# Spreading the side work of a merged four-layer kernel over the attention steps, and group norm two steps earlier

## The reference

```
x = x + L0(gn(x))   # an mLSTM block plus a linear branch, a 3x3 convolution, batch norm, leaky relu
x = x + L1(gn(x))   # attention with 6 heads
x = x + L2(gn(x))   # deformable depthwise 3x3
x = x + L3(gn(x))   # 1x1 to 510, patch transform 2x2, depthwise 3x3, gelu gate, 1x1 back

L1: xq = tokens @ preproj.T + b;  theta = pi * tanh((xq - mean) / std)     # 6 angles for a token
    zq, zk = expectation values of two 6-qubit circuits on theta
    q, k = layernorm(zq @ Wq.T), layernorm(zk @ Wk.T)                        # 4 values each
    attn = softmax(-(|q|^2 + |k|^2 - 2 q.k) / tau)                           # 1024 x 1024 for a head
    out = gate * attn @ v
L2: offsets = conv3x3(x);  out = sum over 9 taps of w[c, tap] * bilinear(x, position + offset[tap])
```

## Time and profile before

| | us |
|---|---|
| median of 3 runs | 8774.78 (8744.1 to 8776.88) |
| profiled execution | 8783.56 |
| its span, first to last instruction | 8781.7 |
| mean granted TensorE clock | 0.922 |
| TensorE busy (matmul) | 7681.9 |
| VectorE busy | 5722.6 |
| ScalarE busy | 3843.6 |
| GpSimd busy | 2158.7 |

### The profile page before, as it was taken

One profiled execution on the slowest core, in us unless ns is written; L12 is line 12 of the kernel. 1 busy time (PEld: TensorE's weight loads), 2 busy tenths in 40 slices (PEclk: granted clock), 3 DMA queues, 4 the chain that ended last, 5 costly groups with the idle time before them and its releaser, 6 DMA issues.

```text
span 8781.7 us, 99875 instructions
## 1 busy us (share of the span) xinstructions
PE 7681.9 (87%) x37116; PEld 3793.0 (43%) x37116; DVE 5722.6 (65%) x9725; ACT 3843.6 (44%) x7430; POOL 2158.7 (25%) x1798
## 2 busy tenths in 40 slices
PE   7999999999999957798988888888888988888877
PEld 4555555555555522344344344343343343343343
DVE  4676666676676734676676676675676676676664
ACT  4555555555555525434435425434334434344320
POOL 1122222222222200214213224123124123133152
PEclk9999999999999978798898999998998999999989
DMA  1111111111111120344434444444444444444365
GB/s 64 37 37 42 46 49 43 40 37 42 43 53 43 37 72 4 103 114 149 130 104 156 125 116 153 130 117 153 116 132 153 115 133 153 110 133 150 110 189 140
DMA packets 244228, 850.01 MB, mean 97 GB/s; under 512 B 46412, under 2 KB 49176, under 8 KB 243360
## 3 DMA queue, kind: packets, MB, share of 16 engines
q1 hardware_dynamic: 150272, 388.71, 16.4%
q0 software_dynamic: 92160, 453.06, 16.3%
q10 hardware_dynamic: 1312, 1.87, 0.1%
HBM read 602.10 MB, written 89.68 MB: 79 GB/s over the span
## 4 chain that ended last, share of the span: by engine, by line
PE 43%; DVE 12%; issue 4%; ACT 4%; DMA 3%; SPq 1%; POOL 0%; another core or an unknown queue 0%; ACTq 0%; DVEq 0%; POOLq 0%
PE ps L2246 9%; PE ps L2481 5%; PE ps L2698 5%; DVE arena L1931 4%; PE ps L2235 4%; PE ps L389 3%; PE ps L2677 3%; PE ps L2168 2%; PE ps L2709 2%; PE ps L2152 2%; PE ps L2365 2%; DMA arena<-img,arena 1%; PE ps L2211 1%; SPq L2732 1%; PE ps L2463 1%
## 5 line engine op out<-in xcount | busy, mean ns | idle before, releaser
L2514 POOL DMA_INDIRECT arena<-img,arena x1152 | 1361.1, 1181 | 2889.2 <-DMA img<-arena 1744.6
L2409 DVE SCALAR_TENSOR_TENSOR arena<-arena 128x384 f32<-128x384 f32 x1152 | 750.0, 651 | 571.6 <-DMA arena<-img,arena 524.8
L1931 DVE TENSOR_REDUCE arena<-ps 128x2 f32<-128x1024 f32 x768 | 894.7, 1217 | 329.6 <-PE ps L2211 326.7
L2090 ACT ACTIVATE arena<-ps 128x512 f32<-128x512 f32 x1536 | 827.3, 600 | 507.5 <-PE ps L2235 341.0
L2246 PE MATMUL ps<-arena 128*64 128x512 f32 x3072 | 904.1, 671 | 0.0
L998 POOL TENSOR_TENSOR arena<-arena 128x512 f32<-128x512 f32 x384 | 443.8, 1162 | 1761.1 <-DMA arena<-decay 1760.8
L2698 PE MATMUL ps<-arena 128*64 128x512 f32 x3072 | 793.3, 639 | 72.2 <-ACT arena L2658 38.2
L2481 PE MATMUL ps<-arena 128*96 128x128 f32 x4608 | 608.9, 289 | 139.3 <-DVE arena L2398 139.3
L2481 PEld LDWEIGHTS ps<-arena 128*96 128x96 f32 x4608 | 557.6, 173 | 321.7 <-issue 319.9
L2235 PE MATMUL ps<-arena 32*128 32x512 bf16 x1536 | 409.5, 409 | 188.1 <-issue 121.9
L964 PE MATMUL ps<-arena 128*128 128x512 f32 x1152 | 507.2, 596 | 0.0
(11 more groups left out here) (349 smaller groups left out, 12720.7 us busy)
## 6 DMA issues: line engine op xcount, KB each, us to landing
arena<-arena SPq DMA_DIRECT2D x1024, 144.5 KB
arena<-decay SPq DMA_DIRECT2D x384, 256.0 KB, 3.2
img<-arena SPq DMA_DIRECT2D x162, 384.0 KB, 2.6
arena<-img,arena POOLq DMA_INDIRECT x1152
arena<-y SPq DMA_DIRECT2D x16, 768.0 KB, 6.4
arena<-x SPq DMA_DIRECT2D x16, 768.0 KB
out<-arena SPq DMA_DIRECT2D x16, 768.0 KB
arena<-x SPq DMA_DIRECT2D x16, 512.0 KB, 5.1
```

Source lines behind the costliest of these rows:

```text
L1931: dve.tensor_reduce(out, self.wides[B.at("max", b, g, n, h) // 2].rearrange("p (a b) -> p a b", a=2), AX.X, AL.max).then_inc(*S.mark("max_ ...
L2090: act.activation(self.p[n % 6], B("score", b, n)[:, :], ACT.Exp).then_inc(*S.mark("p_act", b, n))
L2409: dve.scalar_tensor_tensor(gb[:, 0:384], gb[:, 384:768], pp[:, 1, n:n + 1], gb[:, 0:384], AL.mult, AL.add).then_inc(*S.mark("corner_x", b, n))
L2514: pool.indirect_dma_start(self.g[n % 6], None, img, bass.IndirectOffsetOnAxis(ap=ii[:, n:n + 1], axis=0)).then_inc(*S.landed(f"{self.tag}g ...
```

## The change

Five numbers move, and the digits of PACE. The group norm of the next image is stepped from t = 44 on, no longer from t = 46, on all three engines. `dve_add` goes from t = 44 to t = 42, `act_affine` from t = 40 to t = 38, where it comes behind `finish(0)`. In PACE the sums over all 128 steps stay as they were (185, 155, 172), and in the string of images 2 to 14 also those up to steps 8 and 88; the digits of steps 1 to 7 (in the strings of images 2 to 14 and of the last), of steps 78 to 85 and of steps 88 to 127 are new. From t = 14 on there is one side step for each step (in the last image two from t = 37 on). No instruction is added or removed.

```diff
@@ Layer1.dve
             if t == 39:
                 finish(0)
-            if t == 44:
+            if t == 42:
                 self.dve_add(dve, b + 1)
-            if t > 45:
+            if t > 43:
                 next(gn, None)
@@ Layer1.act
             if t == 38:
                 finish(0)
-            if t == 40:
+            if t == 38:
                 self.act_affine(act, b + 1)
-            if t > 45:
+            if t > 43:
                 next(gn, None)
@@ PACE
 PACE = ("0304040433303700013600007001109209996000400000000007020621002011"
-        "2053100202000000033643000000000000002411100100901000000412000010",
-        "0202020222201010201423061000504220400010401121212314223330012011"
-        "1331111003000000033300000000082000200411100101710100000403000002",
-        "0202020222200020101234070200043200320123000222112134223321012011"
-        "1502111021000000034270000010000000241330013320500100300501100074")
+        "2053100202000012230000001111111111111111111111111111111111111110",
+        "0112111122201010201423061000504220400010401121212314223330012011"
+        "1331111003000022230000001111111111111111111111111111111111111110",
+        "0112111122200020101234070200043200320123000222112134223321012011"
+        "1502111021000022230000001111111111111111111111122222222222222222")
```

## The result

The changed kernel took 8823.62 us (median, 8790.02 to 8853.5), the kernel before beside it 8785.15 (8744.1 to 8803.38): ratio 1.0047, interval 1.0033 to 1.0062. So the change costs about half a per cent, 38 and 47 us by the medians. The forecast was 8775 us, no change; the range up to 8850 holds the time.

The account below looks back on a forecast made before the run. TensorE, busy 87% of the span, was taken as the bound, with ScalarE and VectorE interlocked in the merged stage. Terms of +0.1 us per image x14 and -4 for image 0 gave -3 in total; forecast 8775 us, range 8715 to 8850.

Parts of the forecast that it names:

- Row blocks earlier: Blocks from t = 4: TensorE waits 1.6 us for the slopes, less regained ring waits; +0.4 us per image, ends -0.9 and +1.9.
- score 31 to next L2115: Attention step 31 to the next image's first transposes: 44.8 us after, 41.4 before, +3.4 per image.
- L2115 to the variance matmul: Next image's start: first transposes find the full clock, so 13.9 us becomes 11.5.
- The first twelve steps: Image's head: a gather issued before L1867 and one corner less bring weigh 4 1.3 us earlier, ends -0.3 and -2.
- image 0: No side work, no weigh to wait for: idle 3.16 us becomes some 1.3, the clock stays up, -4 us once.
- regained ring waits: Row blocks: pairs avoid the waits of threes for their ring of buffers, 0.81 us, with ScalarE's share about 1.2.
- Steps 31 to 44, the new wait: At t = 44 TensorE waits about 5.2 us for weigh 2, bounded by 2 and 8.7.
- The clock: Behind the wait at t = 44 the granted clock falls, costing 3 us more per image, ends 0 and 3.9.
- The image's end: Group norm output comes about 1 us after TensorE's work, before 3.16 us idle; bank wait +0.8; L434's total below 20 us.
- A: Rival, gain without its price: the clock stays up at t = 44; 8722 us; with its kin 0.28.
- B: Rival: the wait at t = 44 grows to 8.7 us and the clock costs 3.9; 8834 us; with its kin 0.30.
- C: Rival: the effect is swallowed by remote waits during the run of gathers and measures as nothing; chance 0.15.

Follow-up runs that it names:

- e11: Changed kernel plus unused matmuls in both new TensorE waits, three at t = 4 and ten at t = 44: 8720.87 us, ratio 0.9963 to the kernel before.
- e1: Changed kernel with the row blocks put back to three each at t = 7, 8, 9: 8756.29 us, ratio 0.9999 to the kernel before.
- e6: Changed kernel plus ten unused matmuls in the wait for weigh 2 at t = 44, on another chip: 8539.58 us, ratio 1.0033 to the kernel before.
- e3: Kernel before with only the change's new step numbers (42, 38, 43), PACE digits as before: 8752.17 us, ratio 0.9998 to the kernel before.
- e8: Changed kernel with blocks and weigh 2 moved back, plus four unused matmuls in two layer 3 places, other chip: 8469.14 us, ratio 0.9955 to the kernel before.
- e12: Changed kernel with row blocks back at t = 7 to 9 and weigh 2 ahead of finish(0): 8686.36 us, ratio 0.9924 to the kernel before.
- e5: Changed kernel with row blocks back at t = 7 to 9 and weigh 2 ahead of finish(0), other chip: 8457.7 us, ratio 0.9933 to the kernel before.
- e7: Changed kernel plus three unused matmuls in the wait for the slopes at t = 4, on another chip: 8575.52 us, ratio 1.008 to the kernel before.

## Why the prediction came out as it did

The time is inside the range, 0.5 to 0.6% above the kernel before where the forecast said none. Most of the sum's terms hold; one fails. With a loss of 0.5 to 0.6% the time lies at the border between "no change" (0.42) and "slower by over 0.5%" (0.30). Measured values are the table's, changed against before in its two pairs of columns:

```
us per image                 forecast   measured      ends given
Row blocks earlier             +0.4    +3.7, +3.6    -0.9 to +1.9
score 31 to next L2115         +3.4    +2.3, +2.4
L2115 to the variance matmul   -2.4    -2.8, -2.8
  the last two together        +1.0    -0.6, -0.4    -2 to +5.4
The first twelve steps         -1.3    -1.7, -1.6    -2 to -0.3
sum of the parts touched       +0.1    +1.4, +1.6
image 0, once                  -4      -2.3, -2.6
```

**Row blocks earlier** is the step that failed. The idle time was as forecast, 1.58 us for 1.6, in all 16 places where L2463 waits. Two things were priced wrong. First, the regained ring waits, 1.2 us: they were read from image 6, and most images have less of them. In the kernel before, 7 of the 13 images have no idle time over 0.3 us at their blocks (image 7 is one, first row below; the earlier trace rows has image 6 with 0.81), and where the clock stays up the stretch has a mean of 17.2 us, only 0.6 above those without a wait (16.6). Of the 26 images in both profiles of the changed kernel the clock stayed up in five, and there it takes 18.3 to 19.6 us, mean 19.0; e11, whose clock always stays up here, has 18.64. So without the clock the term is +1.4 to +1.8: as good as nothing was regained, which by the prediction's own terms makes +1.6 (the end of +1.9 that it gives doesn't follow from them).

Second, the clock: in the other 21 images the stretch takes 19.7 to 23.6 us, most often 22.7, which adds some 2 us to the mean. The prediction looked for a fall of the clock only behind idle stretches of over 3 us, the ones its rows showed, and gave the 1.58 us none. The trace of the kernel before had the sign at the blocks themselves: in image 8 it fell behind 1.83 us (the timeline row and the window of 2 us below; busy, clock, DMA share, GB/s), in image 10 behind 1.29 us. e1 shows the whole term: back at 17.56, and 0.5% of the kernel with it.

```profile
5623.99 2.51 PE L2463 MATMUL ps<-arena 96*128 96x96 f32 x24
...
5959.20 0.55 PE L2463 MATMUL ps<-arena 96*128 96x96 f32 x4 [1.83 <-ACT arena L2443]
```

```profile
5960.00:5962.00 2.00, 2.00 (x9) 0.60 0.82 326
```

The Trainium skill (TensorE: Matmul & The Clock Gate, section A second HAM failure mode: psum-queue depth-cycling) tells of a kernel in which TensorE's micro-idles between groups of matmuls came often enough to make the clock swing. That short idle times can bring the clock down is borne out at t = 4; here a single one of 1.58 us in an otherwise busy stretch was enough, in 21 of 26 images. The prediction had used another section of that page (HAM oscillation), and only for what a fall costs, not for what brings one.

**Steps 31 to 44, the new wait** held: 5.08 us for 5.2, at t = 44, with VectorE behind `finish(0)` and `dve_add`. The total for L2398 is 199.3 us (forecast some 190). **The clock** behind it was put at 3 us; e6 and e11, which hold it up, get 2.0 to 2.3 from t = 31 to L2115; in the next stretch e6 is 0.5 to 0.6 shorter than the changed kernel and e11 0.4 longer. So the size is about right, and what hides behind ScalarE a little more than thought. For image 6 the sum up to the next L2115 is met to 0.1 us (44.79 for 44.8). That the table has +2.3 and +2.4 for +3.4 comes from image 6 standing for all: the kernel before needs a mean of 41.7 to 42.0 us there for its 41.4, the changed one 44.1 to 44.2. These 1.0 to 1.1 us, and 0.4 at L2115 to L2128, hide part of what the blocks cost more.

**The image's end** held: L434's total 16.6 us (below 20), 0.95 us of idle and then 0.39 for the bank, where about 1 and 0.8 were expected. **The first twelve steps** held, the head's wait 8.40 to 7.01.

**Image 0** gained about half of what was forecast, 2.3 and 2.6 us for 4 (from its first L2115 to the variance matmul of image 1). Its end became 2.3 to 3.0 us shorter and the head of image 1 3.8 to 4.3, but t = 31 to 44 grew by 5.0 and 3.4: the affine at t = 38 leaves ScalarE no room, and without side work TensorE has nothing to cover it. The prediction had looked at this place only in images with taps. e3 is the same error on a larger scale, made again after the prediction: it was expected to be faster.

The parts touched come to 13 x 1.5 = 20 us. The whole merged stage is 30 us longer in the one pair of profiles (from the first L2115 to the end, 5609.8 against 5579.3) and 38 in the other (5579.2 against 5541.6), the medians 38 and 47. The rest lies in the last image and behind it (7 and 3 us) and, in images 2 to 14, from L2141 to the attention (+2.9, +0.9 per image), with the wandering stretch t = 10 to 26 beside it (-2.2, +0.4); images 0 and 1 together are 3 us shorter in one pair and 3 longer in the other. From L2141 to the attention the changed code does nothing different. The length of that stretch takes a few values, near 183.8, 187 and 189.5 us, with the clock behind idle times of 1.7 to 2.4 us that are not the change's. Two of them from TensorE's timeline of the changed kernel, images 7 and 8, with the window of 2 us behind each:

```profile
5518.00 1.08 PE L2698 MATMUL ps<-arena 128*64 128x512 f32 x4 [2.39 <-ACT arena L2658]
...
5855.35 1.98 PE L2698 MATMUL ps<-arena 128*64 128x512 f32 x4 [2.38 <-ACT arena L2658]
```

```profile
5518.00:5520.00 2.00, 2.00 (x10) 1.00 0.94 215
...
5856.00:5858.00 2.00, 2.00 (x8) 0.50 0.70 141
```

The same idle time, once with and once without a fall. That a shift of a microsecond elsewhere decides which image falls is likely but not shown: e8, which was to fill these gaps, filled the 1.7 us and not the 2.39, and the stretch stayed at 187.6 us.

**Rivals.** A, the gain without its price, did not happen, but its reason is real: e12 has those gains without the two waits and reaches 0.9924, e11 with the waits and without the clock 0.9963. (A said 8722 us, 0.994.) B, a longer wait, did not: the longest for L2398 is 8.0 us and those at t = 44 are about 5. C, that all is swallowed by the gather run, is refuted by the control and the intervals: 0.5% shows through. Its concern about the size of the wandering was right for single profiles.

## What to carry to other kernels

Price a wait of TensorE as idle time plus the clock, also when it is only 1.5 us long and the stream around it is full; look at the granted clock behind such a wait in every image, not in one, since it falls in some and not in others. Where a wait can't go, a few unused matmuls of its length can win back much of its price (here 0.9%, against 1.3% for taking the two waits away); but try them in all such places at once, since filled at t = 4 alone the clock fell at the next short wait, and put them where they don't delay what ends the wait. When a long operation moves on an engine that feeds TensorE, look at the place with the least side work around it, not at the typical one; and of a change in several parts, try each part taken back: here two parts of three cost, and what was left without them was worth 0.8%.

## What the runs showed of the hardware that was not expected

- The same kernel takes 8754.76 to 8785.15 us on the first chips and 8515.24 us on another, 3% less. Almost all of the difference is one stretch, t = 10 to 26, while GpSimd's gathers start: 37 to 40 us per image on the one, 24.2 to 24.5 on the other. The stretch of image 6 in e5 (other chip) and in e12 (the same program, first kind of chip), all engines:

```profile
5179.75:5203.91 24.16, 24.11 (x105) 6.07 (x104) 12.95 (x24) 21.68 (x41) 16.40 (x16) 1.00 0.88 289
```

```profile
5264.20:5305.42 41.22, 30.21 (x104) 6.61 (x103) 17.48 (x34) 22.37 (x41) 23.23 (x22) 0.75 0.76 245
```

  TensorE does the same 104 or 105 matmuls. With e12 the waits of ScalarE's exponentials for "remote" are there (108.5 us in 42 waits; in other runs 85.2 to 144.0), with e5 to e8 the view has no such line. What ScalarE waits for is not settled; no run was made for it. What was to be learnt of the change doesn't hang on it: e5 and e12 give the same ratio.
- The clock's fall at t = 4 lasts in one of two lengths: 3.4 us or 10.2 us (stretch near 19.8 or 22.7), in the same kernel and execution.
- The same idle time can bring the clock down in one kernel and not in another: 0.95 and 0.39 us at L2115 did in 13 of 14 images of e7 and in none of e6, on one chip.
